# The low halves of the up weights on VectorE instead of GpSimd, in the last expert stage

## What is computed

```python
gate = jnp.einsum('bsd,ed->bse', x, Wg) + routing_bias
_, top_idx = jax.lax.top_k(gate, K)                       # K = 4 of E = 8
...
h1 = jnp.einsum('bsd,ehd->ebsh', x, W1)
h2 = jnp.einsum('bsd,ehd->ebsh', x, W2)
eo = jnp.einsum('ebsh,edh->ebsd', jax.nn.sigmoid(h1) * h1 * h2, W3)
out = out + jnp.einsum('ebsd,bse->bsd', eo, weights)
```

## Times and profile before

| | us |
|---|---|
| median of three runs | 2198.45 |
| the profiled execution | 2205.24 |
| its span | 2203.4 |
| start of the stage of the change, about | 1567 |
| pack 1 starts on TensorE | 1595.46 |
| pack 38, the last, starts on TensorE | 2143.81 |

### The profile page before, as it was taken

One profiled execution on the slowest core, in us unless ns is written; L12 is line 12 of the kernel. 1 busy time (PEld: TensorE's weight loads), 2 busy tenths in 40 slices (PEclk: granted clock), 3 DMA queues, 4 the chain that ended last, 5 costly groups with the idle time before them and its releaser, 6 DMA issues. The chain is left out here.

```text
span 2203.4 us, 38903 instructions
## 1 busy us (share of the span) xinstructions
PE 1618.1 (73%) x13182; PEld 1262.8 (57%) x13182; DVE 1422.0 (65%) x2628; ACT 704.8 (32%) x1457; POOL 798.5 (36%) x956
## 2 busy tenths in 40 slices
PE   5956766499975768622948996599588888888881
PEld 3545644377752445411634563488588888888881
DVE  4844555666646655541247885566498888888886
ACT  2311011245531434410312664111244444444440
POOL 1421103620014300103314301188566666666660
PEclk8978788689987887855968997699799999999995
DMA  3464615443116332291225321221355445544525
GB/s 103 161 176 124 184 46 148 157 122 114 48 58 184 73 69 68 61 307 61 63 67 170 104 81 37 68 92 66 140 179 177 155 164 177 173 152 171 181 100 191
DMA packets 286765, 274.02 MB, mean 124 GB/s; under 512 B 59033, under 2 KB 263676, under 8 KB 280958
## 3 DMA queue, kind: packets, MB, share of 16 engines
q1 hardware_dynamic: 274647, 249.09, 36.5%
q0 software_dynamic: 8688, 21.16, 2.7%
q10 hardware_dynamic: 3264, 1.57, 0.4%
HBM read 194.74 MB, written 79.35 MB: 124 GB/s over the span
## 5 line engine op out<-in xcount | busy, mean ns | idle before, releaser
L89 PE MATMUL psum<-e_x_split,e_up_split 128*128 128x256 f32 x2340 | 342.5, 300 | 103.7 <-POOL e_up_split L1788 103.7
L89 PEld LDWEIGHTS psum<-e_x_split,e_up_split 128*128 128x128 f32 x2340 | 319.7, 206 | 110.8 <-issue 87.9
L787 DVE TENSOR_REDUCE a_maxima<-psum 128x2 f32<-128x512 f32 x384 | 257.4, 687 | 160.1 <-PE psum L578 91.9
L1788 POOL TENSOR_TENSOR e_up_split<-e_up_raw,e_up_split 128x512 fp32r<-128x512 f32 x195 | 261.0, 1339 | 214.7 <-ACT e_up_split L1710 213.7
L758 ACT ACTIVATE a_probs<-psum 128x512 f32<-128x512 f32 x384 | 224.8, 598 | 265.6 <-PE psum L600 171.2
L1680 PE MATMUL psum<-e_down_split,e_hidden_split 128*128 128x256 f32 x1170 | 183.5, 295 | 0.8 <-DVE e_down_split L1745 0.8
L1731 ACT ACTIVATE e_silu<-psum 128x256 f32<-128x256 f32 x195 | 75.1, 385 | 325.2 <-PE psum L89 325.2
L1680 PEld LDWEIGHTS psum<-e_down_split,e_hidden_split 128*128 128x128 f32 x1170 | 163.1, 201 | 1.0 <-DVE e_hidden_split L1767 1.0
L578 PE MATMUL psum<-s_k_stack,s_q_stack 96*128 96x256 bf16 x512 | 123.0, 295 | 42.2 <-DMA a_rel_stack<-scr_r 30.0
L1767 DVE TENSOR_TENSOR e_hidden_split<-e_hidden,e_hidden_split 128x256 fp32r<-128x256 f32 x195 | 138.8, 712 | 6.7
L1039 DVE TENSOR_TENSOR a_products<-psum,mask 128x512 f32<-128x512 f32 x128 | 82.9, 686 | 77.6 <-PE psum L972 77.4
(11 more groups left out here) (246 smaller groups left out, 3170.6 us busy)
## 6 DMA issues: line engine op xcount, KB each, us to landing
e_up_raw<-in_w_ffn SPq DMA_DIRECT2D x39, 1280.0 KB, 7.5
e_down_raw<-in_w_ffn SPq DMA_DIRECT2D x39, 640.0 KB, 4.1
scr_q<-p_parts SPq DMA_DIRECT2D x40, 384.0 KB, 2.7
scr_k<-p_parts SPq DMA_DIRECT2D x40, 384.0 KB, 2.8
a_q_stack<-scr_q SPq DMA_DIRECT2D x96, 128.0 KB, 2.9
s_q_stack<-scr_q SPq DMA_DIRECT2D x96, 128.0 KB, 2.7
s_k_stack<-scr_k SPq DMA_DIRECT2D x96, 128.0 KB, 2.7
a_k_stack<-scr_k SPq DMA_DIRECT2D x84, 128.0 KB, 3.0
```

The lines of the kernel that those rows point to most:

```text
L89: last = eng.matmul(out, lhs(a, k), rhs(b, k), start=i == 0, stop=i == len(terms) - 1)
L787: dve.tensor_reduce(MX[:, u // 8, :, u % 8], s_bank(u), AX.X, ALU.max).then_inc(S["s_used"], 1)
L1788: pool.tensor_tensor(SU[:, r, 1, q], RU[:, r, q], SU[:, r, 0, q], ALU.subtract).then_inc(S["up_lo"], 1)
```

## The change

`low_up` moves from GpSimd's program to VectorE's. On VectorE it stands behind `low_down` of the same chunk, and ahead of `take_out` and `low_x`. The five pieces of pack 0 stand first in VectorE's program, ahead of `low_x(0)`. Operation, operands, waits and the semaphore `up_lo` are as they were. GpSimd keeps the row numbers and the scatters.

```diff
@@ VectorE
+                def low_up(i, m):
+                    r, q = i % 2, slice(m * UP, (m + 1) * UP)
+                    dve.wait_ge(S["up_hi"], i * n_h + m + 1)
+                    dve.tensor_tensor(SU[:, r, 1, q], RU[:, r, q], SU[:, r, 0, q], ALU.subtract).then_inc(S["up_lo"], 1)
...
+                for m in range(n_h):
+                    low_up(0, m)
                 low_x(0)
...
                         low_down(i, m)
+                        if i + 1 < packs:
+                            low_up(i + 1, m)
                         if m == LAG and i:
                             take_out(i - 1)
@@ GpSimd
-                def low_up(i, m):
-                    r, q = i % 2, slice(m * UP, (m + 1) * UP)
-                    pool.wait_ge(S["up_hi"], i * n_h + m + 1)
-                    pool.tensor_tensor(SU[:, r, 1, q], RU[:, r, q], SU[:, r, 0, q], ALU.subtract).then_inc(S["up_lo"], 1)
...
-                for m in range(n_h):
-                    low_up(0, m)
                 take_ids(0)
                 take_ids(1)
                 for i in range(packs):
                     for m in range(n_h):
-                        if i + 1 < packs:
-                            low_up(i + 1, m)
                         if i and m >= n_h - HALVES:
```

## The result

The changed kernel takes 2250.8 us (median of 4 runs, 2246.98 to 2258.82); the kernel before took 2198.13 in the same session (4 runs, 2196.65 to 2206.12). The ratio is 1.0237, 95% interval 1.0199 to 1.0275: the changed kernel is slower, by 2.0 to 2.8%. In a later experiment one of ten executions took 7212 us at a mean granted clock of 0.21, against 2200.6 to 2209.9 for the other nine (the version with 24 added matmuls); nothing here says why, and the ratio given there is without it.

A forecast was written before the change was run, and what follows sets the result against it. TensorE's wait once per pack for GpSimd's last low half was taken as the bound, beside clock loss. Pack distances +32.7, clock +12.2 and start -2.4 sum to +42.5 us: 2241 us from 2198.45, range 2206 to 2266.

The forecast's parts named there:

- The wait changes hands and stays at the first chunk: TensorE's wait at each pack's first chunk passes from GpSimd's to VectorE's low half and grows from 2.47 to 3.33 us.
- The low half: Making one low half of the up weights on VectorE takes 0.69 us, 0.61 from start to start, against 1.29 on GpSimd.
- The timetable of VectorE: VectorE's five chunks of a pack start at 2.13, 4.28, 6.84, 10.18 and 12.33 us; the last low half ends at 14.56.
- The distance: Undisturbed first chunks of successive packs lie 14.71 us apart instead of 13.85: 0.86 us for each of 38, +32.7 us.
- nothing waits for: GpSimd, left with two scatters of about 1 us and two small copies a pack, delays no other engine.
- The clock: TensorE runs at half speed after nine pauses in ten, 1.44 us each: 1.30 us a pack instead of 0.97, +12.2 us.
- The start: Before the first matmul, VectorE makes the first five low halves sooner than GpSimd did: -2.4 us.
- VectorE's blocks are no term: GpSimd's blocking of VectorE, 3.8 us in pack 1, goes; the timetable already leaves it out, so nothing is added.
- The last pack: The last pack splits no weights and all after it is as before: 0 us.
- VectorE keeps up: Rival: VectorE isn't late at chunk 4 (lateness under 0.35 us), so the kernel gets faster, about 2165 us; chance 0.08.
- No change: Rival: VectorE's timetable holds but TensorE's clock stays up, 2193 us; chance 0.09 with values between it and the forecast.
- Nothing overlaps: Rival: 0.69 instead of 0.61 us per chunk on VectorE, half-speed stretch at every pause, 2261 us; chance 0.20 with beyond.

## Why the prediction was right, and where it was not

The forecast was 2241 us, range 2206 to 2266; the result is 2250.8. The direction, the place of the wait and the larger term are as worked out. By its steps:

- **The wait changes hands and stays at the first chunk.** Right: all 37 in the earlier trace rows are now L1750's. The pause is 3.53 instead of 3.33.
- **The low half: 0.69 us, 0.61 from start to start.** 0.685 at the median; 0.61 to 0.60 in pack 14 (1807.31, 1807.92).
- **The timetable of VectorE.** The prediction put its chunks at 2.13, 4.28, 6.84, 10.18 and 12.33 behind the pack's start. In pack 14 they are at 2.11, 4.25, 6.84, 10.17 and 12.30. All of it holds, up to chunk 4. The wait in chunk 1 is there too: L1772 starts 4.99 behind, predicted about 5.0.
- **The distance, 14.71 and 14.90 measured.** Here a sentence was wrong: "nothing waits for" GpSimd. The two scatters had been put at no cost because nobody needs their result; but the second one meets the conversion of chunk 4 and makes it 0.24 us longer. With the scatters moved the distance is 14.66. By the form of the term: +0.86 was predicted, +1.05 measured, 0.2 x 37 = 7 us. The Trainium skill, page SBUF — State Buffer, section SBUF: two separate sides, has a note that descriptors of a DMA issued by GpSimd can't be written while a VectorE copy between fp32 SBUF tiles has the shared ports. This conversion has its input and its output in SBUF, and the longer scatter, 1.45 in place of 0.98, agrees with it. That the ports are what the two meet at isn't shown here; the runs show that both are longer, and that the 0.24 us goes with the meeting.
- **The clock: +12.2 predicted, +9.0 measured.** The size is near by luck; the reasoning is not right. I argued that a pause a third longer brings a half-speed stretch behind nine pauses in ten, each at 1.44 us. In fact there were 27 in 37, a share like the 25 of before, and each cost 1.22 x 37 / 27 = 1.67 us on average, because five of them lasted about 6.8 us and not 3.4: those are the five distances over 17. That the length of a pause sets the loss isn't borne out either. Ordered by the pause, the losses per pack are 0.97 (2.47 us), 1.06 (2.58), 1.83 (2.69), 1.86 (3.28), 1.22 (3.53): no order. Two kernels with the same distance and pauses of 2.58 and 3.53 lose nearly the same and in nearly the same three-pack pattern; two kernels whose pauses are alike but whose distances differ by 0.8 (2.58 and 2.69) lose 1.06 and 1.83. The distance alone doesn't decide either: in one execution (the late scatters) there are two patterns with one and the same pause and undisturbed distance. What the loss does follow is the time that the clock spends at 0.50. In the order above that is 2.3, 2.4, 4.5, 5.0 and 2.9 us a pack. What sets this time, and which pattern a given kernel makes, stays open.
- **The start: -2.4.** Measured -2.5.
- **VectorE's blocks are no term.** Right: L1774 has a maximum of 445 ns where L1767 had 1468, and the kernel is slower.
- **The last pack: 0.** +1.6, a half-speed stretch in it.

Of the checks that were named: first chunks are at least 14.88 apart; 10 of 37 distances are that, 22 are 16.1 to 16.4 and five 17.2 to 17.6, a little over the 16.0 to 16.3 that I named. The mean clock of the stretch is 0.91 and not 0.88. The 0.88 didn't follow from the prediction's own term: by my estimate 33 half-speed stretches of 3.4 us in some 593 us make 0.905.

Of the rivals, "VectorE keeps up" failed at the named condition: the lateness at chunk 4 is 12.30 - 11.12 = 1.18 us against 0.35. "No change" needed a clock that stays up; the matmuls in the pause made it come true, at 2204.4 us. "Nothing overlaps" was wrong in its cause (0.61 and not 0.69), and that its 2261 isn't far from the result is chance. Its sum was wrong too: in the prediction's own timetable chunks 0 and 1 have room for 0.08 us more, and the last low half counts by its duration, so 0.69 from start to start delays the next pack through chunks 2 and 3 alone, by 0.16 us and not 0.40.

What the prediction did not see is the larger point: it took the place of the low halves as given. From the same rows one could have read that VectorE idles at the start of a pack and is late at its end, and the program loads the next pack's up weights a pack before it splits them (7.6 us from issue to landing at the median, in the trace of the kernel before). Moved up, the same change gives 0.9486.

## What to carry to other kernels

Before moving work to a faster engine, write down that engine's timetable between two deadlines, and place the moved instructions where it has time, not where they stood on the slower one: here the same instructions made +2.4% or -5.1%. Price a pause of TensorE in two terms, the pause itself and the clock that is lost behind it; filling the pause with matmuls that change nothing separates the two (here they gave back 46 us of the changed kernel and 32 of the one before), and a shorter chain can lose at the clock what it gained. An instruction whose result nobody waits for still has a price if an engine on the chain is held while it runs (here 0.24 us a pack).

## What was not expected of the hardware

- Pauses of TensorE of 1.64 us cost no clock in one execution, where the single half-speed stretch stands behind a pause of 2.01 us; pauses of 2.47 to 3.53 us cost between 0.97 and 1.86 us a pack, in no order of the length. The half-speed stretches come in patterns over packs (two of three at an undisturbed distance of 14.9, every one in a row of distances of 17.07, and every one where the undisturbed distance would be 14.06), and they last about 3.4 or about 6.8 us.
- VectorE's conversion of 128x256 and a scatter's issue on GpSimd are both longer when they meet: 0.29 became 0.53 us, 0.98 became 1.45.
- A VectorE operation with one SBUF input, the conversion, is held by GpSimd's subtraction just as one with two (1.35 in place of 0.29).
